# First tile's keys and values stored and gathered apart, loads reordered, first moments by tile

## Reference

```python
kv = kv_src @ Wkv.T; k, v = jnp.split(kv, 2, axis=-1)
gather = seg_id[:, :, None] - jnp.arange(4)
k_sel = kh[b_idx, :, gc]; v_sel = vh[b_idx, :, gc]
probs = softmax(where(gather < 0, -inf, einsum(qh, k_sel) * 0.25))
x = x + tanh(g_xattn) * (einsum(probs, v_sel) @ Wo.T)      # q = layernorm(x) @ Wq.T
x = x + tanh(g_ffn) * experts(layernorm(x))                # 8 experts, top 2, 256 -> 1024 -> 256
```

## Time and profile before

| what | value |
|---|---|
| median of 3 runs | 353.91 us (353.19 to 354.49) |
| profiled execution, its own time | 353.07 us |
| its span, first to last instruction | 351.2 us |
| granted TensorE clock, mean | 0.986 |
| PE / DVE / POOL / ACT busy | 92% / 76% / 59% / 50% |

### The profile page before, as it was taken

The page is one execution under the profiler, slowest core; times in us unless marked ns, Lnnn a source line. Parts: engine busy times, 40 slices in busy tenths (PEclk is TensorE's granted clock), DMA queues, the critical chain, the costliest instruction groups (busy, mean ns, idle before and its releaser), DMA issues.

```text
span 351.2 us, 11438 instructions
## 1 busy us (share of the span) xinstructions
PE 322.4 (92%) x3486; PEld 265.9 (76%) x3486; DVE 268.2 (76%) x629; ACT 174.2 (50%) x490; POOL 207.7 (59%) x227
## 2 busy tenths in 40 slices
PE   8698999999898799999999999999999999999930
PEld 7467888888797687888888888888888887778710
DVE  4769999999998867878787788877887785665520
ACT  2452455555466267465656555565656633243400
POOL 3486889996762250748557576576574774662330
PEclk9999999999999999999999999999999999999995
DMA  7799999998999420233223323133232423231210
GB/s 245 244 350 417 405 418 401 417 401 331 360 381 379 141 65 19 37 60 47 48 37 60 63 34 63 33 63 55 41 47 49 63 36 59 39 66 23 35 20 12
DMA packets 31422, 53.23 MB, mean 152 GB/s; under 512 B 4850, under 2 KB 25570, under 8 KB 29316
## 3 DMA queue, kind: packets, MB, share of 16 engines
q0 software_dynamic: 9408, 26.63, 29.7%
q1 hardware_dynamic: 16628, 22.46, 17.8%
q10 hardware_dynamic: 5328, 3.37, 3.1%
HBM read 42.29 MB, written 10.17 MB: 149 GB/s over the span
## 4 chain that ended last, share of the span: by engine, by line
PE 67%; DVE 20%; issue 4%; POOL 2%; ACT 2%; DMA 1%; ACTq 0%; POOLq 0%; DVEq 0%
PE ps L1134 29%; PE ps L1148 16%; PE ps L1151 8%; DVE ps L1317 5%; PE ps L1162 2%; DVE sel L1313 2%; PE ps L1156 2%; DVE w_parts L1313 2%; PE ps L911 2%; DVE xs L1349 1%; PE ps L1155 1%; PE ps L1150 1%; PE ps L970 1%; DVE rden L1336 1%; PE ps L883 1%
## 5 line engine op out<-in xcount | busy, mean ns | idle before, releaser
L1134 PE MATMUL ps<-sel,w_parts 128*128 128x128 f16 x1776 | 141.7, 219 | 1.0 <-issue 0.8
L1134 PEld LDWEIGHTS ps<-sel,w_parts 128*128 x1776 | 119.4, 98 | 26.3 <-issue 1.8
L862 ACT ACTIVATE sel<-ps,b1T 128x128 f32<-128x128 f32 x296 | 84.3, 368 | 90.4 <-PE ps L1134 89.2
L627 POOL DMA_INDIRECT out<-sel x37 | 63.2, 1709 | 84.3 <-DVE sel L1599 69.8
L1148 PE MATMUL ps<-w_parts,sel 128*128 x259 | 96.4, 379 | 0.4
L1151 PE MATMUL ps<-w_parts,sel 128*128 x259 | 70.6, 273 | 0.0
L1554 DVE SCALAR_TENSOR_TENSOR sel<-sel 128x512 f16<-128x512 f32 x74 | 51.3, 693 | 2.5
L619 POOL DMA_INDIRECT sel<-tokens_split,sel x37 | 43.4, 1174 | 15.9 <-DVE sel L1522 9.3
L1540 DVE SCALAR_TENSOR_TENSOR w_parts<-w_parts (+1 forms) x32 | 39.0, 1220 | 10.0 <-issue 5.9
L614 POOL TENSOR_TENSOR sel<-sel 128x1 f32<-128x1 f32 x37 | 40.4, 1091 | 2.9 <-PE ps L1162 2.8
L1552 DVE TENSOR_SCALAR sel<-sel 128x512 f16<-128x512 f32 x74 | 33.1, 447 | 9.9 <-ACT sel L862 9.6
(11 more groups left out here) (230 smaller groups left out, 462.9 us busy)
## 6 DMA issues: line engine op xcount, KB each, us to landing
w_parts<-in_L_ffn_w SPq DMA_DIRECT2D x16, 1024.0 KB
out<-xs SPq DMA_DIRECT2D x16, 128.0 KB
tokens_split<-xsplit ACTq DMA_DIRECT2D x13, 128.0 KB
xs<-in_x ACTq DMA_DIRECT2D x2, 512.0 KB, 7.9
xs<-in_x SPq DMA_DIRECT2D x2, 512.0 KB, 7.2
near_rows<-w_parts SPq DMA_DIRECT2D x4, 256.0 KB, 6.1
sel<-tokens_split,sel POOLq DMA_INDIRECT x37
out<-sel POOLq DMA_INDIRECT x37
```

What stands on the lines that cost most here:

```text
L627: pool.indirect_dma_start(out_rows, bass.IndirectOffsetOnAxis(slot_row[:, at(q - 1)], 0), y_sb[(k + 3) % 4], None, compute_op=ALU.add).the ...
L862: act.activation(h32[n][:, c * P:c * P + P], ps_h[n][:, c * P:c * P + P], ACT.Silu, bias=biases[:, c:c + 1], scale=1.0 / (X_SCALE * W_SCALE))\
L1134: mm = pe.matmul(ps_h[n][:, c * P:c * P + P], w, xx, start=(i == 0), stop=(i == len(products) - 1))
```

## The change

Tile 0 gets keys and values of its own: `keys_of(0)` and `values_of(0)` are two halves of `sel0`, filled by two gathers of 128 x 1024 (512 KB each) from `k_first` and `v_first`, which ACT stores by itself as soon as each half (128 x 256) is made. The key half of Wkv is turned and multiplied first. Tokens of tile 0 are loaded apart; tokens of batches 1 and 2, the gates and the small biases move to SP's queue, and those of batch 3 are issued when the keys of tile 0 are there. The first moments are taken for tile 0, then 1 to 3, then 4 to 11 in the prologue, and for 12 to 15 inside steps 1, 2 and 3. GpSimd's `first_norms` are now for 1, 3, 8 and 4 tiles instead of 4 and 12, the last one in iteration 5; the split of b2 moves to its iteration 2. Wo is turned apart from Wq, and `query(1)` stands before the keys and values of batches 2 and 3.

```diff
@@ sync
-            sp.wait_ge(s["wkv_in"], 16)
+            tokens_in(1)
             tokens_in(2)
...
+            sp.dma_start(b1_raw, b1.rearrange("e (c p) -> (e c) p", p=P)).then_inc(s["small_in"], 16)
+            sp.dma_start(gate_raw, gate_w).then_inc(s["small_in"], 16)
+            sp.dma_start(b2_raw, b2).then_inc(s["b2_in"], 16)
...
-                sp.wait_ge(s["kv_ok"], b + 1)
+                sp.wait_ge(s["kv_ok"], b + 2)
                 sp.dma_start(kv_near[b], kv_sb[:, b, :]).then_inc(s[f"kv_out{b}"], 16)
                 if b == 0:
+                    sp.wait_ge(s["sel_k"], 16)
                     tokens_in(3)
@@ gpsimd
-            first_norms(1, slice(0, TPB))
+            first_norms(1, slice(0, 1))
+            first_norms(2, slice(1, TPB))
...
-            gather(0, TPB)
-            first_norms(2, slice(TPB, T))
-            pool.wait_ge(s["b2_hi_ok"], 1)
...
+            with pool.If(general < 1):
+                pool.wait_ge(s["kv_out_k"], 16)
+                pool.indirect_dma_start(sel0[:, 0:WIN * D], None, k_first, bass.IndirectOffsetOnAxis(win_near[:, 0:1], 0))\
+                    .then_inc(s["sel_k"], 16)
+                pool.wait_ge(s["kv_out_v"], 16)
+                pool.indirect_dma_start(sel0[:, WIN * D:2 * WIN * D], None, v_first,
+                                        bass.IndirectOffsetOnAxis(win_near[:, 0:1], 0)).then_inc(s["sel_v"], 16)
...
+            gather(1, 2)
+            first_norms(3, slice(TPB, 3 * TPB))
+            gather(2, TPB)
             for t in range(T - 1):
...
+                if t == 2:
+                    pool.wait_ge(s["b2_hi_ok"], 1)
+                    pool.tensor_scalar(b2_raw[:, :], b2_raw[:, :], 16.0, None, ALU.mult).then_inc(s["b2_lo_ok"], 1)
+                    pool.wait_ge(s["b2_lo_ok"], 1)
+                    pool.tensor_tensor(b2_lo[:, :], b2_raw[:, :], b2_hi[:, :], ALU.subtract).then_inc(s["b2_lo_ok"], 1)
...
+                if t == 5:
+                    first_norms(4, slice(3 * TPB, T))
@@ scalar
-            act.activation(WkvT[:, 0, :], ps[:, 2, :], ACT.Copy).then_inc(s["wkvT_ok0"], 1)
+            act.activation(WkvT[:, 0, 0:D], ps[:, 2, 0:D], ACT.Copy).then_inc(s["wkvT_ok0"], 1)
+            act.wait_ge(s["wkvT_ps"], 2)
+            act.activation(WkvT[:, :, D:2 * D], ps[:, 1, :].rearrange("p (k c) -> p k c", k=KC), ACT.Copy)\
+                .then_inc(s["wkvT_ok0"], 1)
+            for h in range(2):
+                act.wait_ge(s["kv_ps"], h + 1)
+                act.activation(kv_sb[:, 0, D * h:D * h + D], kv_halves[h], ACT.Copy).then_inc(s["kv_ok"], 1)
+                act.wait_ge(s["kv_ok"], h + 1)
+                act.dma_start((k_first, v_first)[h], kv_sb[:, 0, D * h:D * h + D])\
+                    .then_inc(s[("kv_out_k", "kv_out_v")[h]], 16)
...
+            first_x(0)
@@ tensor
-            spin(18)
+            spin(8)
...
-            spin(12)
+            spin(4)
@@ vector
-            first_norm(3)
...
+                if 0 < t < 4:
+                    dve.wait_ge(s["x_in3"], 16)
+                    first_norm(3 * TPB + (t if t > 1 else 0), 3 * TPB + t + 1)
                 if added:
                     residual(t - 2)
```

More of the change, by code:

```diff
@@ L266, in flamingo_layer @@
         ps_tile = ps[:, 3, :]
-        kv_bank = [ps[:, i, :] for i in (4, 5, 6, 7)]
+        kv_bank = [None, ps[:, 4, :], ps[:, 7, :], ps[:, 4, :]]
+        kv_halves = [ps[:, 4, 0:D], ps[:, 5, 0:D]]
         ps_x16 = ps[:, 0, :].bitcast(F16)
@@ L300, in slot, with keys_of, values_of, norm_group @@
                 .rearrange("p (j c) -> p j c", j=WIN)
+        def keys_of(u):
+            return slot(u)[:, :, 0:D] if u else sel0[:, 0:WIN * D].rearrange("p (j c) -> p j c", j=WIN)
+        def values_of(u):
+            return slot(u)[:, :, D:2 * D] if u else sel0[:, WIN * D:2 * WIN * D].rearrange("p (j c) -> p j c", j=WIN)
+        def norm_group(u):
+            return 1 if u < 1 else 2 if u < TPB else 3 if u < 3 * TPB else 4
         def tiles_in(t, *lags):
@@ L529, in gather @@
                     for u in range(first, last):
-                        if u % TPB == 0:
+                        if u == 1 or u >= TPB and u % TPB == 0:
                             pool.wait_ge(s[f"kv_out{u // TPB}"], 16)
@@ L650, in _, with first_x @@
             act.wait_ge(s["wkvT_ps"], 1)
-            act.activation(WkvT[:, 0, :], ps[:, 2, :], ACT.Copy).then_inc(s["wkvT_ok0"], 1)
+            act.activation(WkvT[:, 0, 0:D], ps[:, 2, 0:D], ACT.Copy).then_inc(s["wkvT_ok0"], 1)
[8 more added lines that the diff above has]
+                    .then_inc(s[("kv_out_k", "kv_out_v")[h]], 16)
+            def first_x(u):
+                act.wait_ge(s["shift1_ok"], norm_group(u))
+                wait(act, "xnT_ps", u - 1)
+                act.activation(xn[:, u % 2, :], xs[:, u, :], ACT.Identity, scale=rstd1[:, u:u + 1],
+                               bias=shift1[:, u:u + 1]).then_inc(s["xn_ok"], 1)
+            act.wait_ge(s["segt_ps"], 1)
+            act.wait_ge(s["seg_top_ok"], 1)
+            first_x(0)
             general = flag(act)
@@ L665, in keys_values @@
             def keys_values(b):
-                act.wait_ge(s["kv_ps"], b + 1)
+                act.wait_ge(s["kv_ps"], b + 2)
                 act.activation(kv_sb[:, b, :], kv_bank[b], ACT.Copy).then_inc(s["kv_ok"], 1)
-            keys_values(0)
-            def first_x(u):
-                act.wait_ge(s["shift1_ok"], 1 if u < TPB else 2)
-                wait(act, "xnT_ps", u - 1)
-                act.activation(xn[:, u % 2, :], xs[:, u, :], ACT.Identity, scale=rstd1[:, u:u + 1],
-                               bias=shift1[:, u:u + 1]).then_inc(s["xn_ok"], 1)
             def first_turned(u):
@@ L912, in keys_values @@
                 mm.then_inc(s["kv_ps"], 1)
-            for n in range(2):
-                pe.wait_ge(s[f"wkvT_ok{n}"], 1)
-            keys_values(0)
+            pe.wait_ge(s["ctxT_ok"], 1)
+            pe.wait_ge(s["wkvT_ok1"], 1)
+            for h in range(2):
+                pe.wait_ge(s["wkvT_ok0"], h + 1)
+                for c in range(KC):
+                    mm = pe.matmul(kv_halves[h], ctxT[:, 0, c, :], WkvT[:, c, D * h:D * h + D],
+                                   start=(c == 0), stop=(c == KC - 1))
+                mm.then_inc(s["kv_ps"], 1)
             general = flag(pe)
@@ L1016, in _ @@
             context_turn(3, 2, 0).then_inc(s["ctxT_ps"], 1)
+            first_turn(1)
+            pe.wait_ge(s["wo_in"], 16)
+            weight_turn(wo_raw, 7)
             keys_values(1)
-            first_turn(1)
+            query(1)
             pe.wait_ge(s["wT_ok"], 2)
@@ L1025, in _ @@
             pe.transpose(ps[:, 3, 64:64 + E * FC], b1_raw, ident[0:E * FC, 0:E * FC]).then_inc(s["small_ps"], 1)
-            query(1)
             first_turn(2)
             pe.wait_ge(s["small_T"], 2)
-            pe.wait_ge(s["kv_ok"], B)
+            pe.wait_ge(s["kv_ok"], B + 1)
             for t in range(1, T - 1):
@@ L1289, in _, with first_norm @@
             v.tensor_scalar(general_i[:, :], seg_max[:, :], float(P), None, ALU.is_ge).then_inc(s["seg_flag"], 1)
-            dve.wait_ge(s["wkvT_ps"], 1)
-            v.tensor_copy(WkvT[:, 1, :], ps[:, 3, :]).then_inc(s["wkvT_ok1"], 1)
-            def first_norm(b):
-                dve.wait_ge(s[f"x_in{b}"], 16)
-                for t in range(TPB * b, TPB * b + TPB):
+            def first_norm(first, last):
+                for t in range(first, last):
                     v.bn_stats(st1[:, t, :], xs[:, t, :]).then_inc(s["stats1"], 1)
-                for t in range(TPB * b, TPB * b + TPB):
+                for t in range(first, last):
                     dve.wait_ge(s["stats1"], t + 1)
                     v.bn_aggr(mv1[:, t, :], st1[:, t, :]).then_inc(s["aggr1"], 1)
-            first_norm(0)
-            first_norm(1)
-            first_norm(2)
-            first_norm(3)
+            dve.wait_ge(s["x_first"], 16)
+            first_norm(0, 1)
+            for b in range(3):
+                dve.wait_ge(s[f"x_in{b}"], 16)
+                first_norm(max(TPB * b, 1), TPB * b + TPB)
             def step(t):
```

93 lines of the change are left out of this document (58 added, 35 removed).

## The result

| what | before | after |
|---|---|---|
| median | 353.81 us (353.19 to 354.49, 8 runs) | 357.06 us (355.87 to 358.42, 8 runs) |
| ratio to before, 95% interval | | 1.0092 (1.0072 to 1.0111) |
| profiled execution, its own time | 353.07 us | 357.38 us |
| its span | 351.2 us | 355.7 us |
| granted TensorE clock, mean | 0.986 | 0.973 |

The account below looks back on a forecast made before the run. The prediction took ScalarE's exponentials of tile 0 to bound the start and VectorE the steps from 4 on. Its terms, -0.8 + 1.6 + 1.1 = +1.9 us on the median of 353.91, gave 355.8 us, range 353.0 to 357.6.

Parts of the forecast that it names:

- What bounds the kernel now: Step 0: ScalarE's exponentials of tile 0 end the last wait, the gather 0.61 us behind; VectorE sets pace from step 4.
- Term 1: Prologue: the exponentials of tile 0 come earlier, -0.8 us (bounds -0.4 and -1.1); the faster gather is hidden.
- Term 2: VectorE's steps 1 to 3: four tiles of moments moved inside cost +1.6 us (bounds 1.4 and 1.8).
- Term 3: GpSimd's norms moved into iteration 5 make VectorE wait in steps 7 and 8: +1.1 us (bounds 0.3 and 2.0).
- (c): Rival: batch 3's tokens land over 10.3 us after issue and VectorE waits 1.5 us in step 1: 357.3 us; chance 0.15.
- The sum: Whole kernel: the three terms add to +1.9 us, which added to the median gives 355.8 us.
- (a): The forecast itself: all three terms hold, 355.0 to 356.8 us; chance 0.5.
- (b): Rival: GpSimd's lateness is absorbed, Term 3 is 0, sum +0.8, 354.7 us; chance 0.2, including no effect at all.
- (d): Rival: tile 0's exponentials don't wait for batches 2 and 3, batch 3's copy starts before 18.7: 352.2 us; chance 0.15.

Follow-up runs that it names:

- e1: Changed kernel with ten more TensorE spins behind the turn of Wq and twelve behind `first_turn(0)`: 357.27 us, ratio to before 1.0123.
- e2: Changed kernel with `query(1)` back behind the small weights' turns, as before: 356.54 us, ratio to before 1.0105.
- e7: Kernel before with only the moments of tiles 12 to 15 put in steps 1 to 3 and their norms in iteration 5: 356.75 us, ratio 1.0088.
- e11: Changed kernel with batch 3's tokens loaded right behind the first store of near rows: 356.84 us, ratio to before 1.0100.
- e12: Kernel of e10 with batch 3's tokens loaded right behind the first store of near rows: 355.82 us, ratio to before 1.0071.
- e4: As e3, with GpSimd's norms for the last twelve tiles and the b2 operations also back in the prologue: 354.89 us, ratio to before 1.0044.
- e3: Changed kernel with all moments back in the prologue and batch 3's tokens loaded behind batch 2's: 356.07 us, ratio to before 1.0079.
- e10: Changed kernel with tile 0's keys and values stored and gathered together again: 359.29 us, ratio to before 1.0144.
- e8: Kernel before with ScalarE's exponentials of tile 0 moved ahead of tanh, expert-bias copy and centring of tile 3: 353.39 us, ratio 1.0001.
- e9: Changed kernel with tile 0's split undone, moments and norms moved back early, batch 3's tokens early, e1's spins and e2's order: 353.34 us, ratio 0.9976.

## Why the prediction was right or wrong

**What bounds the kernel now** was half right. ScalarE's exponentials do end the last wait of step 0, and what the gather wins is idle time: 0.61 us of it before, 2.64 after. What I did not look for is the next thing that falls due: the gather of tile 1. It had landed by 24.86 in the kernel before and no wait named it, so I took the exponentials to be the only limit. e1 shows that with them out of the way it is the next limit: t1 stayed at 25.15.

**Term 1** is the step that failed. I forecast -0.8 us and bounds of -0.4 to -1.1; the exponentials moved by -0.02 and the product of tile 1 by +0.34. `first_x(0)` came at 10.04, a microsecond sooner than my 11.0. But the keys and values of batch 1 began at 16.16 where I had 15.15. The clock stood at half for some 3 us: the query cost 1.97 and the six turns 1.49 us, where I had written "fewer spins, unless the granted clock falls" among the things that cost nothing and gave it no chance and no price. That alone cost more than the 0.8: in e1, with the clock at 1.00, the exponentials came at 22.21, 1.7 us sooner than before and 0.9 sooner than I had forecast. The order with `query(1)` ahead costs another 1.08 us (e2), but that was in my sum with 1.0. Even so the term would not have been won: with the exponentials sooner, t1 stayed at 25.15, behind tile 1's gather (e1). The +0.34 at tile 1 is again something else, which goes with the moments in the steps (e7) and which I had not seen. The split was on the list as an early gain that is hidden; e11 and e12 show that it costs 1.0 us by itself, and I had no price for it on tile 1. Its gather took 4.44 us, as I had taken (4.3), but went at 13.80 and not at 12.7, since the key store needed 4.8 us to land.

**Term 2** was forecast at +1.6 and measured 1.55 in the changed kernel and again in e7. The third of a microsecond ahead of tile 1's product comes on top.

**Term 3** was forecast at +1.1. The norms in iteration 5 cost 1.10 (e7, and e4 against e3), with waits in steps 7 and 8 as described. The changed kernel has 2.18. The other 1.08 are the late gather of tile 4 (e11), whose cause I had in hand in rival (c), but with another victim: batch 3's tokens did not make VectorE wait in step 1; they stood ahead of batch 1's store, and GpSimd waited. In (c) I had asked only who needs the tokens, not who stands behind them on their queue.

**The sum.** -0.8 + 1.6 + 1.1 became +0.34 + 1.55 + 2.18 + 0.42 in the profiled executions. The last 0.42 are spins that TensorE ran at half clock ahead of the first expert turn; the table by stretches has it at 0.50 from 122 to 124 us. Spins and turn, before and after:

```profile
117.39 4.18 PE L883 MATMUL ps<-ones 128*128 128x128 f16 x72
122.89 0.40 PE L1162 MATMUL ps<-ident,sel 128*128 128x128 f16 x4 [1.32 <-DMA sel<-tokens_split,sel]
121.52 5.80 PE L934 MATMUL ps<-ones 128*128 128x128 f16 x72
127.38 0.38 PE L1230 MATMUL ps<-ident,sel 128*128 128x128 f16 x4
```

The spins took 1.6 us longer and outlasted the DMA that the turn had waited for. The clock was at 0.50 there in e1 too, and the stretch from t13 took 41.78 us; with 1.00 it took 41.0 to 41.5 in all others but e10. Of the medians' 3.25 us, term 2 and the norms make 2.65; that I was 1.3 us too low is term 1 and the tokens' place, less what other executions than the profiled one give back. The direction was right because the two terms that carried it were right. That the number fell into the range is in part luck: 357.06 lies above the 355.0 to 356.8 of my forecast (a) and inside the range only because I had widened it for (c), which did not happen.

**Rivals.** (b), absorbed lateness, is refuted by e4 against e3. (c) missed narrowly: the tokens landed 10.0 us after their issue at 18.16, at 28.2, just before VectorE took them at 28.39; I had set the limit at 10.3. (d) is refuted by 22.37, where the copy of batch 3's keys still started.

What stays open: why the clock falls in some profiled executions and not in others, what slows the second half gather, what widens the stretch ahead of tile 1's product, and why e10 spreads over 4 us. e12 ties e10's excess to the place of batch 3's tokens (3.5 us between the medians, which are of two chips; 3.1 when each is set against its kernel before), but the profiled execution of e10 shows only 1.7 us of it (spans of 355.3 and 353.6), nearly all in the wait before the first expert turn, and why a load at 20 us should be felt there isn't shown.

## What to carry to other kernels

When a chain of waits names one releaser, list what comes due within the next microsecond for the operations behind it, DMA landings too: with the exponentials 1.7 us sooner, the next gather made VectorE wait 1.94 us. A load that is moved needs two questions, who waits for it and what stands behind it on its queue; here the second cost 1.1 us of the steady steps, though moving the load alone (e11) did not shorten the whole. Work moved from idle time ahead of a steady loop into the loop of the engine that sets its pace costs all of its duration that no wait covers (1.55 us here, for moments that last 0.87, 0.55 and 0.55 us in steps 1 to 3, with a wait left only in step 1), and on a second, nearly full engine about half of it (1.10 of 2.0 us).

## What the hardware showed unexpectedly

The fall of the granted clock is not told by how busy TensorE had been. Busy 0.44 of 2 us from 10 to 12 us, the changed kernel fell to 0.50 from 12.3 us on, e2 with 0.44 too, and e11 with 0.44 did not; 0.44 from 12 to 14 us left the kernel before at 1.00, 0.48 and 0.62 were followed by 0.50 in e7 and e8. The Trainium skill, page "TensorE: Matmul & The Clock Gate", "Part 1", says that a hardware block sets the clock by how busy TensorE has recently been; the four falls named here all follow poorly filled stretches, but such stretches are no sufficient sign. At half clock the same query took 1.97 instead of 1.10 us.

Halving the pieces of a gather did not halve its time: from issue to use it took 4.44 us after (512 KB), 5.58 before and 5.95 in e9 (1 MB). Some 2 us of each pass before the first byte, whatever the size: in e9 the DMA engines moved nothing from 15 to 16 us, with the gather issued at 14.25; after, nothing from 14 to 15 us and 0.05 MB from 15 to 16, with the issue at 13.80.

A store of 256 KB on SyncE's queue took 12.6 us to land behind 512 KB of tokens while gathers ran (after). In the kernel before, the first of these stores, ahead of all gathers, took 2.6 us, and the second, beside gathers but with no tokens ahead, 9.6: most of the time is the gathers', not the tokens'.
